# The first stage of a four-layer kernel on Trainium2: another order of its steps, its statistics and its mask test

## The reference

```
xn = _ln(x, ln1_w, ln1_b)
sx = _token_shift(xn, state[:, i1])
xxx = jnp.tanh((xn + sx * maa_x) @ maa_w1).reshape(b, l, 5, 1, EXTRA_MAA)
xxx = jnp.matmul(xxx, maa_w2).reshape(b, l, 5, E)
x5 = xn[:, :, None] + sx[:, :, None] * (maa_stack + xxx)
w = jnp.exp(-jnp.exp(time_decay + jnp.tanh(x5[:, :, 1] @ decay_w1) @ decay_w2))
r = x5[:, :, 3] @ Wr.T
k = x5[:, :, 0] @ Wk.T
v = x5[:, :, 2] @ Wv.T
g = jax.nn.silu(x5[:, :, 4] @ Wg.T)
```

## Time and profile before

| | us |
|---|---|
| median of 3 runs | 5328.55 |
| lowest and highest | 5319.98, 5329.23 |
| the profiled execution, its own time | 5320.13 |
| its span in the profile | 5318.5 |

### The profile page before, as it was taken

The page is one execution under the profiler, slowest core; times in us unless marked ns, Lnnn a source line. Parts: engine busy times, 40 slices in busy tenths (PEclk is TensorE's granted clock), DMA queues, the critical chain, the costliest instruction groups (busy, mean ns, idle before and its releaser), DMA issues. The chain is left out here.

```text
span 5318.5 us, 75415 instructions
## 1 busy us (share of the span) xinstructions
PE 4723.6 (89%) x28818; PEld 1691.3 (32%) x28818; DVE 3735.3 (70%) x4684; ACT 2931.1 (55%) x5418; POOL 2013.1 (38%) x912
## 2 busy tenths in 40 slices
PE   5886998998688799997899999997789999996899
PEld 2332444443233233332322222221333333331344
DVE  6768999998453677772499999994567777771421
ACT  3553444444232366664288888886326666665432
POOL 0116666665000388885000000000008888886000
PEclk9897999999799799999999999998899999998999
DMA  2334434343220433322211111111424232212100
GB/s 99 125 138 132 116 103 114 112 113 89 92 65 33 89 69 69 69 57 97 87 29 32 32 32 33 33 33 47 134 87 99 58 77 61 65 45 76 64 24 16
DMA packets 474865, 391.90 MB, mean 74 GB/s; under 512 B 175151, under 2 KB 372628, under 8 KB 474472
## 3 DMA queue, kind: packets, MB, share of 16 engines
q1 hardware_dynamic: 474496, 387.00, 26.6%
HBM read 246.50 MB, written 139.34 MB: 73 GB/s over the span
## 5 line engine op out<-in xcount | busy, mean ns | idle before, releaser
L2803 DVE TENSOR_REDUCE att_part<-att_scores 128x2 f32<-128x802 f32 x1024 | 953.4, 986 | 108.6 <-PE att_scores L2642 96.8
L2776 ACT ACTIVATE att_prob<-att_lower 128x512 f32<-128x512 f32 (+1 forms) x1664 | 883.5, 596 | 128.4 <-PE att_lower L2656 107.4
L3610 DVE TENSOR_REDUCE att_part<-att_scores 128x1 f32<-128x423 f32 x1280 | 675.8, 590 | 219.3 <-PE att_scores L3313 219.2
L3554 ACT ACTIVATE att_prob<-att_lower 128x512 f32<-128x512 f32 (+1 forms) x1088 | 563.3, 602 | 243.9 <-PE att_lower L3325 242.0
L3594 POOL TENSOR_TENSOR att_acc<-att_acc,att_prob 128x1024 f32<-128x1024 f32 (+2 forms) x240 | 671.1, 2796 | 51.8 <-ACT att_prob L3554 22.6
L2379 DVE TENSOR_REDUCE att_part<-att_scores 128x1 f32<-128x401 f32 x1024 | 515.4, 567 | 161.9 <-PE att_scores L2193 161.7
L1373 POOL TENSOR_TENSOR scan_z<-scan_r,scan_states 128x512 f32<-128x512 f32 x256 | 469.6, 1839 | 337.4 <-DVE scan_states L1450 323.2
L2671 PE MATMUL att_lower<-att_prob,att_v 128*32 128x256 f32 (+1 forms) x6144 | 523.6, 413 | 19.7 <-issue 19.7
L2318 ACT ACTIVATE att_prob<-att_scores 128x512 f32<-128x512 f32 (+1 forms) x832 | 430.8, 601 | 195.3 <-PE att_scores L2205 195.2
L2790 POOL TENSOR_TENSOR att_out<-att_sums_sb,att_spread 128x512 f32<-128x512 f32 x32 | 40.7, 1272 | 1164.1 <-DMA att_spread<-recips 1164.1
L2359 POOL TENSOR_TENSOR att_acc<-att_acc,att_prob 128x1024 f32<-128x1024 f32 (+2 forms) x176 | 450.2, 2558 | 68.8 <-ACT att_prob L2318 56.4
(11 more groups left out here) (431 smaller groups left out, 7896.4 us busy)
## 6 DMA issues: line engine op xcount, KB each, us to landing
v<-scan_val SPq DMA_DIRECT2D x96, 256.0 KB, 2.3
att_v<-v SPq DMA_DIRECT2D x32, 768.0 KB
att_spread<-recips SPq DMA_DIRECT2D x64, 256.0 KB
mix_plane<-in_mask SPq DMA_DIRECT2D x16, 800.5 KB, 6.5
att_k<-k1hi SPq DMA_DIRECT2D x32, 400.2 KB
att_k<-k3hi SPq DMA_DIRECT2D x32, 400.2 KB
scan_x<-in_ctx_t SPq DMA_DIRECT2D x12, 1024.0 KB, 5.7
o<-att_out SPq DMA_DIRECT2D x32, 256.0 KB, 2.0
```

The costliest lines, as they stand in the source:

```text
L2776: nc.scalar.activation(prob[g % NP][0:kw(kt), h, :], scores2[0:kw(kt), n % RING2, :], ACT.Exp).then_inc(exped, 1)
L2803: nc.vector.reduce_max(part[q % 2][:, :, ec, piece], scores1[:, bank["unit", p], :, 0:PIECE], AX.X).then_inc(reduced, 1)
L3554: nc.scalar.activation(prob[g % NP][0:kw(kt), h, :], scores2[0:kw(kt), n % RING2, :], ACT.Exp).then_inc(exped, 1)
L3610: nc.vector.reduce_max(part[q % 2][:, hc, piece:piece + 1], scores1[:, bank["piece", p], 0:PIECE], AX.X).then_inc(reduced, 1)
```

## The change

The constants' phase loses its block and its barrier. Its loads follow the first load of x on SP; its six passes over the mask rows go to DVE between the parts of batch 0's statistics, with the row buffers lying where lerp 2 and 3 are allocated, so that ACT's drains of mix23 wait for the stores of the rows.

In the list, mix23 and mix4 of a batch stand directly behind each other, ahead of its decay1; the next batch's mean stands behind decay1, its std behind decay2. The deviation is taken per token on four columns: PE multiplies four 128x128 pieces of the squares, as the stationary side, with one column of 1/512, ACT takes the root of 128x4 numbers, DVE the reciprocal of these (`invert`), and a new step, spread, brings them back to 512 columns in all partitions by four products with the identity; ACT drains that.

The planes are reduced on ACT, one pass with the absolute value and a sum per plane, behind value 0, value 2, recept 1 and recept 3; two planes are loaded behind value and two behind gate. The value's low half moves from DVE to POOL, ahead of the low half of mixing 4. DVE's loop is written out instead of walking the list. Here is the core of the diff (of DVE's loop the new lines alone):

```diff
-    loaded, made, step, stored = ph.sem("loaded"), ph.sem("made"), ph.sem("step"), ph.sem("stored")
...
-            sp.wait_ge(made, 1)
-            for name, row in (("km1", row1), ("km3", row3)):
-                for g in range(w[name].shape[1]):
-                    sp.dma_start(w[name][:, g, :], row[:]).then_inc(stored, 16)
-            sp.wait_ge(stored, 16 * 2 * QUAD)
-
...
-            dve.wait_ge(loaded, 16 * 4)
-            link(nc.vector.tensor_scalar(k["headmean"][:], k["head"][:], 1.0 / HS, None, ALU.mult))
-            for m, row in ((m8, row1), (m32, row3)):
-                link(nc.vector.tensor_copy(keep[:], m[:]))
-                link(nc.vector.tensor_scalar(keep[:], keep[:], 0.0, MASKED, ALU.not_equal, ALU.mult))
-                link(nc.vector.tensor_scalar(row[:], keep[:], MASKED, None, ALU.subtract))
-            nc.vector.memset(m8[:], 0).then_inc(made, 1)
-    ph.renew()
...
@@ -206,20 +176,24 @@
         def order():
             yield 0, "mean", range(1)
             yield 0, "std", range(1)
+            yield 0, "spread", range(1)
             yield 0, "lora", range(2)
             yield 0, "mix10", range(2 * C)
-            yield 0, "mix23", range(2 * C)
             for b in range(B):
                 more = b + 1 < B
+                yield b, "mix23", range(2 * C)
+                yield b, "mix4", range(C)
                 yield b, "decay1", range(1)
+                if more:
+                    yield b + 1, "mean", range(1)
                 yield b, "key", range(C)
                 yield b, "decay2", range(C)
                 if more:
-                    yield b + 1, "mean", range(1)
-                yield b, "value", range(C)
+                    yield b + 1, "std", range(1)
+                yield b, "value", range(0, 2)
                 if more:
-                    yield b + 1, "std", range(1)
-                yield b, "mix4", range(C)
+                    yield b + 1, "spread", range(1)
+                yield b, "value", range(2, C)
                 yield b, "recept", range(C)
                 if more:
                     yield b + 1, "lora", range(2)
@@ -227,8 +201,6 @@
                 if more:
                     yield b + 1, "mix10", range(2 * C)
                 yield b, "gate", range(2, C)
-                if more:
-                    yield b + 1, "mix23", range(2 * C)
             yield B - 1, "masks", range(1)
 
         ends, total = {}, 0
...
@@ -250,13 +222,22 @@
 
                 def load_plane(j):
                     if j >= 2:
-                        sp.wait_ge(reduced, 2 * (j - 1))
+                        sp.wait_ge(reduced, j - 1)
                     sp.dma_start(plane[j % 2][:], w["mask2"][j // C, j % C * P:(j % C + 1) * P, :]).then_inc(ploaded[j % 2], 16)
 
                 def load_weight(sem, dst, src):
                     sp.dma_start(dst, src).then_inc(wloaded[sem], 16)
 
+                def send_row(i, name):
+                    sp.wait_ge(rowsmade, i + 1)
+                    for g in range(w[name].shape[1]):
+                        sp.dma_start(w[name][:, g, :], row[i][:]).then_inc(rowsent, 16)
+
                 load_x(0)
+                sp.dma_start(k["ident"][:], w["c_ident"]).then_inc(constants, 16)
+                sp.dma_start(k["head"][:], w["c_head"]).then_inc(constants, 16)
+                sp.dma_start(m8[:], w["mask1"]).then_inc(maskrows, 16)
+                sp.dma_start(m32[:], w["mask3"]).then_inc(maskrows, 16)
                 for dst, src in ((lnw, "ln1_w"), (lnb, "ln1_b"), (mx, "maa_x"), (td, "time_decay"), (stack, "maa_stack")):
                     sp.dma_start(dst[:], w[src]).then_inc(small, 16)
                 sp.dma_start(prev[:], w["prev1"].rearrange("b p c -> p b c")).then_inc(small, 16)
@@ -272,6 +253,8 @@
                 load_plane(0)
                 load_plane(1)
                 planes = 2
+                send_row(0, "km1")
+                send_row(1, "km3")
                 for b in range(B):
                     for what in OUTS:
                         sp.wait_ge(drained, ends[b, what])
@@ -279,7 +262,7 @@
                             sp.wait_ge(decayed, b + 1)
                         n = out_index(b, what)
                         sp.dma_start(w[OUTS[what][1]][b].rearrange("c p t -> p c t"), y[n % 2][:]).then_inc(stored[n % 2], 16)
-                        for _ in range({"value": 1, "recept": 1, "gate": 2}.get(what, 0)):
+                        for _ in range({"value": 2, "gate": 2}.get(what, 0)):
                             if planes < PLANES:
                                 load_plane(planes)
                                 planes += 1
@@ -295,6 +278,7 @@
                     sp.wait_ge(stored[i], 16 * 5 * B // 2)
                 sp.wait_ge(vstored, 32 * B)
                 sp.wait_ge(flagged, 16)
+                sp.wait_ge(rowsent, 16 * 2 * QUAD)
 
             @block.tensor
             def _(pe):
...
+                    if group.j >= 8:
+                        pe.wait_ge(drained, group.j - 7)
+                    for j in range(T // P):
+                        ins = nc.tensor.matmul(psum[:, group.j % 8, j * P:(j + 1) * P], rowinv[:, j:j + 1].broadcast_to([P, P]),
+                                               k["ident"][:], start=True, stop=True)
+                    ins.then_inc(product, 1)
+                    group.j += 1
+
                 for b, what, part in order():
                     if what == "mean":
                         pe.wait_ge(totalled, 2 * b + 1)
                         group([(k["mean"][:], sq[:, 0, :])])
                     elif what == "std":
                         pe.wait_ge(totalled, 2 * b + 2)
-                        group([(k["mean"][:], sq[:, 0, :])])
+                        square_means()
+                    elif what == "spread":
+                        pe.wait_ge(inverted, b + 1)
+                        spread_rows()
                     elif what == "lora":
                         if b == 0:
                             pe.wait_ge(wloaded["w1"], 16)
...
+                    nc.scalar.activation(plane[j % 2][:], plane[j % 2][:], ACT.Abs, accum_out=extremes[:, j:j + 1]).then_inc(reduced, 1)
+                    seen_planes += 1
+
                 act.wait_ge(small, 16 * 6)
                 for b, what, part in order():
                     if what == "mean":
                         if b:
                             act.wait_ge(centred, b)
                         drain(mean[:], ACT.Identity)
+                        if b:
+                            lerp_high(b - 1, 2)
                         act.wait_ge(centred, b + 1)
                         nc.scalar.activation(sq[:], x[b % 2][:], ACT.Square).then_inc(squared, 1)
                     elif what == "std":
                         if b:
+                            act.wait_ge(inverted, b)
+                        drain(rowstd[:], ACT.Sqrt, n=T // P, bias=k["eps5"][:])
+                    elif what == "spread":
+                        if b:
                             act.wait_ge(shifted, b)
-                        drain(rstd[:], ACT.Sqrt, bias=k["eps5"][:])
+                        drain(rstd[:], ACT.Identity)
                     elif what == "lora":
                         if b:
                             act.wait_ge(product, ends[b - 1, "mix4"])
...
@@ -402,6 +424,8 @@
                             act.wait_ge(half234, 3 * b)
                         elif b:
                             act.wait_ge(half234, 3 * b - 1)
+                        elif what == "mix23":
+                            act.wait_ge(rowsent, 16 * 2 * QUAD)
                         if what == "mix23":
                             lerp_high(b, 0)
                         for c in range(C):
...
                                 drain(dst[:, o, :], ACT.Silu if what == "gate" else ACT.Identity, scale=1.0 / WSCALE)
-                                for i in {("key", 0): (2,), ("key", C - 1): (3,), ("recept", 2): (4,)}.get((what, o), ()):
-                                    lerp_high(b, i)
-                            if what == "value":
+                                if what == "key" and o == 0 and b == B - 1:
+                                    lerp_high(b, 2)
+                                if (what, o) in (("value", 0), ("value", 2), ("recept", 1), ("recept", 3)):
+                                    plane_sum()
+                            if what == "value" and part.stop == C:
                                 act.wait_ge(drained, ends[b, "value"])
                                 nc.scalar.activation(vhi[:], dst[:], ACT.Identity).then_inc(vrounded, 1)
+                                lerp_high(b, 4)
 
             @block.gpsimd
             def _(pool):
                 for b in range(B):
                     for i in (2, 3, 4):
+                        if i == 4:
+                            pool.wait_ge(vrounded, b + 1)
```

(96 more changed lines are left out.)

114 lines of the change are left out of this document (31 added, 83 removed).

## The result

The changed kernel takes 5297.8 us, median of 5 runs (5285.5 to 5300.6), against 5328.3 of the kernel before: ratio 0.9942, 95% interval 0.9930 to 0.9954. The forecast was 5288 in a range of 5256 to 5310, "faster" at 0.92. Run again beside fresh runs of the kernel before it took 5295.3 against 5327.6, 0.9931 (0.9914 to 0.9947). So sign and range held; the median lies 10 us above the forecast, and it is worth finding out where the 10 us are, since the first stage alone won more than was forecast.

The account below looks back on a forecast made before the run. No engine was full in the first stage's periods; PE came nearest, its waits being DVE's lateness. Head 17.7, periods 7 and tail 7 sum to 31.7 off the profiled 5320.1: 5288, range 5256 to 5310; later stages priced at nothing.

Parts of the forecast that it names:

- Head: First stage's opening, up to batch 0's mixing 1 and 0 drains, 69.2 us before: 17.7 won, bounds 16 and 19.5.
- Periods: Three batch-to-batch spans between mixing 1 and 0 drains, 252.6 us before: 245.5 forecast, 7 won, bounds 213 to 257.
- bank wait: First period: mix4 waits 6 us for a bank with no gate to cover it.
- lora's wait: Late in a period: POOL's values' split and half of lerp 4 delay DVE's last four operations, so lora waits 3.3 us.
- plane passes of 1.6: ACT's four mask passes over 128x1601 per period: 1.6 us each, costing nothing because hidden by PE.
- the row: Profile windows where PE was busy 4.00 of 4.00 us yet the clock fell from 0.97 to 0.60, against the skill's idle-gap rule.
- Tail: From the last batch's mixing 1 and 0 drains to the last gate drain, 72.2 us before: 65, 7 won, bounds 5 and 11.
- rival 2: Only the head is won: periods 84 each, tail 5, about 23 us won, 5297; chance 0.12.
- Rival 1: PE becomes the bound if POOL's instructions miss DVE's or the clock holds: period 72, time 5255; chance 0.22.
- Rivals 3: Rival 3: slower, clock stays at 1.2 GHz beyond the mixing run, in key behind the long f32 stretch: 5330; chance 0.04.
- Rival 4: Overlap isn't had: barrier's time returns since loads of weights set the head; won 14 at most, 5306; chance 0.07.
- the median's 8.4: Shown runs' median lay 8.4 us above the profiled execution; put into the range's upper bound, not the forecast.

Follow-up runs that it names:

- 18.4 alone: The kernel before with only the constants' phase dissolved as in the change, the walk over the batches left old: 5305.0 us, 0.9954.
- drains first: The changed kernel with ScalarE draining the first half of mixings 2 and 3 before it rounds mixing 0: 5276.7 us, 0.9907.
- mixing 4 late: The changed kernel with mixing 4's product back behind value and its interpolation behind the next batch's shift: 5290.9 us, 0.9937.
- 512 columns: The changed kernel with the deviation again on 512 columns, one product with a constant and no second product: 5304.4 us, 0.9956.
- second pair: Both kernels run again without edit: stage end 405.4 in the kernel before and 368.3 in the changed kernel.
- both edits: The changed kernel with the value's split on VectorE behind the shift and half of mixings 2 and 3 drained before mixing 0's rounding: 5271.0 us, 0.9893.

## Why the prediction was right, and where not

*Head.* Forecast 17.7, measured 18.1, and 18.4 alone. The multiplication by the reciprocal starts at 24.61 (forecast 25.7).

*Periods.* Forecast 245.5 together; 240.6 and 245.5 in the two traces. The working's steps are seen one by one: the bank wait of 6 us in the first period (6.1) and under 1 behind it (0.6), the four last operations stretched by GpSimd, lora's wait of 3.3 (3.65), mixing 4 and decay1 slow in part, plane passes of 1.6 (1.53, and 0.20 for the sum's read). Only the first period was mis-sized, 85.5 against 82.1 and 83.5. The 68.6 us of work at 2.4 GHz add up to 68.7 from the terms given; nothing hangs on it.

*Clock.* The choice between the row and the Trainium skill's rule (TensorE: Matmul & The Clock Gate, section HAM oscillation) was made for the row, and the changed kernel bears that out: with TensorE busy 3.00 of 3.00 us the clock stood at 0.50. But that the long run of f32 products brings the fall isn't shown: in the kernel with drains first the same run kept 3.7 us for mixing 4 and 3.65 for decay1 in three batches. Nor does an idle stretch decide it: behind 2.59 us decay1 took 3.65, 6.20 and 6.26 in the kernel with mixing 4 late. When the clock falls here stays open. What wasn't asked is what the new place of mixing 4 is worth: in the periods it wins nothing, as the run with it late shows (233.2 us for the three), whereas the run with 512 columns (253.6) shows that their 7 to 12 us hang on the deviation per token.

*Tail.* Forecast 65 with 7 won; to the last gate drain 62.7 and 66.1, 9.4 and 6.1 won.

*The split of the values.* Seen rightly, as the cause of lora's wait; it was taken as given that it must stand there. On VectorE, behind the shift, it costs no time in any period: with that edit alone the median was 5282.6 against 5295.3 on the same chip.

*The step that failed* ends the first paragraph of the first part: "Everything behind is the same code in both kernels and is priced at nothing." It cost 8.5 us in the mean, 11.6 in the two executions first compared; the prediction had named a later stage of another length among the signs of its being wrong. The source behind the stage is the same; its semaphore numbers and its place in the instruction stream are not, which accounts for 1.9 us (shown) and about 1.5 (argued); the rest is open.

*Luck.* By medians 30.5 us were won (5328.3 to 5297.8), close to the sum's 31.7, but not because the sum was right: the first stage won 39.3 in the first trace and 37.1 in the second pair, 5 to 8 more than forecast, and the part behind it lost 11.6 and 6.7. Two errors of opposite sign nearly cancel.

*The rivals.* The measured median is the number of rival 2, "only the head is won", and yet that rival is wrong: the periods and the tail are won, and lost elsewhere. Rival 1 is what the change could have been (71.3 per period in the kernel with both edits). Rivals 3 and 4 aren't seen: key ran at its 2.4 GHz level behind the slow stretch, and the barrier's time didn't return. Rival 4 with the median's 8.4 would have been 5314, outside the range that was said to hold it.

## What to carry to other kernels

Price what a change leaves in place of the code around it: instructions and semaphores added in one stage shift the numbers and the code of all later ones, and where clears fall back to one by one, or a block of code lands in a gap, microseconds can appear far from the diff. Check a stage's gain against the whole execution's before trusting either.

When two engines lock each other out, don't move work to the idle one; move it to the idle time of the busy one. And before filling TensorE's wait with other work, add up what that work delays in its new place. Read a clock effect from every batch: one batch alone would have shown a wait that keeps the clock up, and the next two show that it doesn't.

## What the runs showed of the hardware that was not expected

- The clock stood at 0.50 with TensorE busy 3.00 of 3.00 us, in f32 products end to end (changed kernel, second period). In the same products it was 1.00 with 0.64 us of idling ahead of decay1 (drains first, three batches), and with 2.59 us of idling once 1.00 and twice 0.58 (mixing 4 late: 3.65, 6.20 and 6.26 us).
- Clearing 34 semaphores one by one took 2.0 us on SyncE, 60 ns each, where one clear of the whole range took 0.09.
- A store landed 1.6 us later, and SyncE's gap was 1.5 us longer, in the 9 traces in which a packet of instructions on q8 fell into that gap, against the 5 in which none did.
- GpSimd's pass also held up VectorE's operations of one tensor input (the shift's group of four at 5.93 instead of 2.29 us), not only those of two; the reductions weren't held up.
- The same program's first stage took from 359.8 to 368.3 us, and 399.1 to 405.4 before the change: single traces compare parts of a stage to a few us only.
